# A segment-maximum stage whose TensorE makes the node positions one group earlier

## The reference, cut to what matters

```python
def _graph_conv(x, src, dst, ew, W_rel, b_rel, W_root):
    msg = x[src] * ew[:, None]
    agg = jax.ops.segment_max(msg, dst, num_segments=N)
    agg = jnp.where(jnp.isfinite(agg), agg, 0.0)
    return agg @ W_rel.T + b_rel + x @ W_root.T
src, dst = (edge_index[0], edge_index[1])
ew = 1.0 / (pos[src] - pos[dst])
```

## Time and profile before

| what | us |
|---|---|
| median of 3 runs | 6097.28 |
| lowest, highest | 6085.78, 6100.27 |
| the profiled execution, its device time | 6076.85 |
| its span, first to last instruction | 6075.1 |
| mean granted TensorE clock over the span | 0.720 |

### The profile page before, as it was taken

One profiled execution on the slowest core, in us unless ns is written; L12 is line 12 of the kernel. 1 busy time (PEld: TensorE's weight loads), 2 busy tenths in 40 slices (PEclk: granted clock), 3 DMA queues, 4 the chain that ended last, 5 costly groups with the idle time before them and its releaser, 6 DMA issues. The chain is left out here.

```text
span 6075.1 us, 87448 instructions
## 1 busy us (share of the span) xinstructions
PE 3609.1 (59%) x18318; PEld 2628.9 (43%) x18319; DVE 3319.1 (55%) x10385; ACT 1849.9 (30%) x4701; POOL 2684.2 (44%) x2677
## 2 busy tenths in 40 slices
PE   1455555555554454577214997995666666666664
PEld 0444454455532222244001554654555555555552
DVE  6666666666664444587001333225666666666668
ACT  0444444444422222243000000003444444444442
POOL 1555555555526666601774000005555455454524
PEclk9855555555566676687556998997777777777776
DMA  5555555556531111123103885644333333333331
GB/s 116 182 183 190 186 182 188 185 181 194 185 106 50 49 49 49 49 90 84 22 0 64 200 191 186 196 140 115 87 85 84 83 85 85 84 86 82 87 85 33
DMA packets 822107, 695.48 MB, mean 114 GB/s; under 512 B 538545, under 2 KB 717733, under 8 KB 808431
## 3 DMA queue, kind: packets, MB, share of 16 engines
q1 hardware_dynamic: 552746, 449.58, 24.9%
q0 software_dynamic: 97584, 175.68, 10.8%
q10 hardware_dynamic: 171540, 68.00, 4.7%
HBM read 510.64 MB, written 108.55 MB: 102 GB/s over the span
## 5 line engine op out<-in xcount | busy, mean ns | idle before, releaser
L2362 POOL DMA_INDIRECT ring<-xl_rows,idx x880 | 893.0, 1015 | 1681.1 <-DVE idx L2542 861.6
L435 POOL DMA_INDIRECT ringa<-x_sign_pos,idxa x880 | 864.7, 983 | 691.5 <-DVE msga L600 385.0
L987 POOL DMA_INDIRECT edge_counts<-edge_cnt,places x832 | 828.1, 995 | 733.9 <-issue 262.9
L520 PE MATMUL sela<-hota,endsa 128*128 128x128 f32 x1760 | 425.0, 417 | 482.6 <-ACT endsa L461 400.7
L1905 PE MATMUL pss<-x3s,mats 128*128 128x385 bf16 x2401 | 452.5, 340 | 355.3 <-issue 349.3
L2487 PE MATMUL zps<-xr,hotT 128*128 x2640 | 384.2, 254 | 381.1 <-DVE z L2561 212.6
L520 PEld LDWEIGHTS sela<-hota,endsa 128*128 128x128 f32 x1760 | 365.1, 307 | 500.5 <-issue 430.6
L2500 PE MATMUL ops<-val,hot 128*128 128x200 f32 x1760 | 469.6, 417 | 141.9 <-issue 125.5
L2683 DVE TENSOR_TENSOR out<-out,ops 128x200 f32 x880 | 317.9, 361 | 415.5 <-remote 277.0
L2489 PE MATMUL zps<-We,eaT 128*128 128x128 f32 x1760 | 495.3, 367 | 63.0 <-issue 62.4
L2487 PEld LDWEIGHTS zps<-xr,hotT 128*128 128x128 bf16 x2640 | 271.8, 114 | 492.1 <-issue 458.8
(11 more groups left out here) (388 smaller groups left out, 6591.7 us busy)
## 6 DMA issues: line engine op xcount, KB each, us to landing
edge_counts<-zeroa SPq DMA_DIRECT2D x55, 1568.0 KB
matd<-edge_counts SPq DMA_DIRECT2D x12, 6272.0 KB
keyb<-edge_keys SPq DMA_DIRECT2D x50, 1216.0 KB
reseta<-resets SPq DMA_DIRECT2D x110, 512.0 KB
dstba<-dst_in_tile_bf ACTq DMA_DIRECT2D x112, 256.0 KB
dstb<-dst_in_tile_bf SPq DMA_DIRECT2D x110, 256.0 KB
eaT<-in_eaT SPq DMA_DIRECT2D x880, 32.0 KB
val<-in_ea ACTq DMA_DIRECT2D x880, 32.0 KB
```

Source lines behind the costliest of these rows:

```text
L435: p.indirect_dma_start(out=ring[:, k, :], out_offset=None, in_=table, in_offset=bass.IndirectOffsetOnAxis(ap=idx[:, k:k + 1], axis=0)).the ...
L520: ins = t.matmul(sel[q % 2][:, k * P:(k + 1) * P], ends[:, q % 2, k, :], hot[:, q, k, :], start=True, stop=True)
L987: p.indirect_dma_start(out=g.M.rearrange("d s -> (d s)").unsqueeze(1), out_offset=bass.IndirectOffsetOnAxis(ap=g.place[:, c:c + 1], axis=0 ...
L2362: p.indirect_dma_start(out=ring[:, q % GR, k, :], out_offset=None, in_=g.xl_rows[0:N, :], in_offset=bass.IndirectOffsetOnAxis(ap=idx[:, (q ...
```

## The change

TensorE makes the positions of the next group in the middle of its iteration, between the selection and the transposes of messages, instead of those of the current group at its head. The positions of group 0 are made before the loop. One group of positions more is made at the end than is used.

```diff
@@ -543,10 +543,10 @@
                 def body(it):
                     for q in range(NG):
                         G = it * NG + q
-                        positions(G, q)
-                        for lag, stage in ((3, select), (1, transposed), (2, back)):
+                        for lag, stage in ((3, select), (-1, positions), (1, transposed), (2, back)):
                             if not (isinstance(it, int) and q < lag):
                                 stage(G - lag, (q - lag) % NG)
+                positions(0, 0)
                 turns(t, body, TURNS)
                 GL = TURNS * NG
                 select(GL - 3, NG - 3)
```

## The result

The changed kernel takes 6132.8 us (median of 6 runs, 6109.0 to 6150.7) and the kernel before, in the same comparison, 6096.7 us (6 runs, 6085.8 to 6100.3). The ratio is 1.006 with a 95% interval of 1.0037 to 1.0083: slower by about 36 us. So it is slower on all three occasions, by 0.35% to 0.6%.

A forecast was written before the change was run, and what follows sets the result against it. The prediction took the stage as bound by a loop of waits, VectorE's on four TensorE signals that come late while gathers run. Terms -49, +11 and +66 us gave +28 on 6097, so 6125 us; range over all 6025 to 6215.

The forecast's parts named there:

- The wait moves to the selection: VectorE's wait leaves the sum of positions (209.2 us) for the additions; additions plus scan grow from 177 to 300 us or more.
- -49 us for what stays gained: VectorE ahead of the sum of positions: 0.6 us comes back at each of 81 waits; bounds 0 and -138.
- +66 us for 20 long runs: GpSimd's gathers: 20 runs of twelve without a stop, TensorE's signals coming after their end, 3.3 us more each.
- +28 us of the sum: Whole program: the terms -49, +11 and +66 us together, added to the kernel before's time.
- +11 us for TensorE's loop: Position matmuls between selection and transposes put TensorE behind by about 0.1 us in half of 220 steps; bounds 0 and +64.
- GpSimd's waits: GpSimd's waits for messages, 101 for 385 us before, become fewer but longer, more of them near 8 us.
- need not stop: Messages come up to 3.45 us earlier after a long wait, so GpSimd goes on gathering without its stop.
- The clock: TensorE's granted clock, 0.58 in the stage, should stay; if it rose, all of TensorE's terms would shrink.
- (a): Rival: long gather runs do not get longer or cost nothing, sum -38 us, 6059 us; chance 0.22.
- (b): Rival: GpSimd's run and the held signals come 3.4 us earlier at some 45 waits, 153 us, 5944 us; chance 0.08.
- (c): Rival: no change, the wait moves whole to the selection or terms cancel, 6080 to 6115 us; chance 0.24.
- The rule of the Trainium skill: Spoke against the +66 us term: longer gather runs would hold nothing up, leaving a sum of -38 us.

The follow-up runs named there:

- second and third set: Later comparisons, each with its own kernel before (6017 and 6020 us); the changed kernel, run again unchanged, measured 1.0035 in both.
- experiment 4: Kernel before and changed kernel, each with the maximum stage's gathers left out after the first turn's 16: 0.9345 and 0.9329 of the whole kernel before.
- first set: Comparison of the later ring refill, doubled position matmuls and positions behind the transposes against the kernel before, which takes 6091 us there.
- later slots: Kernel before with the ring's slots filled one group later, GpSimd waiting for messages one group nearer: 1.0004 of the kernel before.
- two cut kernels: Kernel before and changed kernel with the maximum stage's gathers left out after the first turn's 16: 5621.1 and 5618.6 us.
- The same edit: Changed kernel with the ring's slots filled one group later: 0.9988, then 1.0022 of the kernel before.
- another 1.002 and 1.0056: Changed kernel with the next group's positions made behind the transposes of messages, ahead of the transposes back: 1.002, then 1.0056 of the kernel before.

## Why the prediction came out

The time was 6132.8 us where I had 6125 us, and slower by more than 0.3% was the likeliest case. The steps one by one:

- **The wait moves to the selection.** Right, though in part to the scan: 45 of the 247 us are ahead of it. Ahead of the sum of positions 1.5 us are left, as said (a few us). The additions and the scan together went from the 177 us of the earlier trace rows to 424 by the same rows after (220.1 + 119.9 + 84.3), past the 300 that I had named.
- **-49 us for what stays gained.** Open. By the booking the changed kernel gains 46 to 68 us in runs of 6 to 10 gathers, but that is a different thing from a gain at each wait, and no run has the gain without the rest. I had it from three waits walked; that the two numbers are near may be luck.
- **+66 us for 20 long runs.** The number was near: 15, 19 and 19 runs of eleven and more (with the one at the start left out), where there had been 2 and 4, so 13 to 15 more. The price was too high: such a run is booked at 3 x 0.70 to 3 x 0.78 = 2.1 to 2.3 us over three mean groups, and not 3.3, so 35 to 41 us. I had taken it from a single run at 8.29 us a group, and the mean is 7.74 to 7.94. That run was misread as well: after its first gather, leave out the next, which starts at 1642.49 after 2.05 us of idleness. So it was one gather, a pause, and eleven in a row. And since the kernel with positions made twice loses without long runs, that they cause the changed kernel's loss is not shown.
- **What the sum left out.** The short runs. Behind a run of eleven or twelve comes one of eight (48 of 53 times in the changed kernel's three traces), and behind that mostly one of four, with its own pause. Such short runs are booked at 17 us more in two profiles and 77 in one. Nothing in my sum stood for that. In the first profile it covered the price that was too high, and that is luck: the +28 us of the sum stands beside 36 measured there and 22 and 24 us in the second and third set, but its terms don't hold one by one.
- **+11 us for TensorE's loop.** Without gathers it is nothing: both orders take 1168 us. With gathers the doubled matmuls cost 14 to 29 us, so some of it may be real there. The two could not be told apart. The 482 us that the prediction gives as TensorE's wait for ScalarE's copy are all idle time ahead of the selection; the copy ends 401 of them. No term hangs on it.
- **GpSimd's waits.** Half right. They became longer: 29 are over 7 us, where 4 were. They did not become fewer: 107 against 101. So GpSimd stops as often as before; "need not stop" failed.
- **The clock.** 0.60 against 0.58, as expected no factor.
- **The rivals.** (a), faster by the gain alone, is out by the time. That long runs cost nothing, its reason, is not refuted as such: they take 7.7 to 8.1 us a group in every trace, in the kernel before too, but no edit tested their price. (b), the shorter loop, is out by its time, though runs of 6 to 10 did get shorter. (c), the same time, was close: 0.35% in the second and third set is just over the bound of 0.3%, which lies inside both intervals.
- **The rule of the Trainium skill**, page "SBUF — State Buffer", section "SBUF: two separate sides", that a DMA and a compute instruction don't slow each other: VectorE's times agree, as its scan takes 1275 ns with gathers and 1274 without. The eight matmuls of the selection are recorded with 2.07 us in both cases too, but their ends are modelled, so that is no test. But by that rule alone no signal of TensorE would come later for the gathers, and in experiment 4 the waits for these signals went away with them. Whether it is their writes to SBUF, their descriptors, the semaphores' own way or matmuls that really end later than the model says was not tried, and stays open.

What stays open besides is the rest of the program. In the first profiles it took 6128.9 - 1613.1 = 4515.8 us in the changed kernel and 4497.3 in the kernel before, 19 us more outside the stage, though nothing there was changed. The other profiles of the first set say the same: 4517 to 4522 us in the three that make positions early, and 4499 in the kernel before with later slots. In the second and third set the same difference was 1 to 9 us. For the two cut kernels it was 12 us between the profiled executions (spans 5629.0 and 5617.1 us, with stages alike), and yet the medians, 5618.6 and 5621.1 us, show none. So I can't say that it belongs to the program. It does mean that of the 36 us of the first comparison a part may lie outside the stage that the prediction is about.

## What to carry to other kernels

Here three orders on TensorE only chose which of its signals was waited for: where all signals of an engine are late at the same times, the wait taken away at one is met at the next. Before such a change, sum the waits for all signals of that engine (here 462 to 548 us of idleness ahead of positions, scan and additions in all twelve traces with gathers, whatever the order, of which 117 are not waits for a signal) and ask what they have in common. In a kernel that runs in a rhythm of long and short runs, the mean of a group hides a gain in one kind and a loss in another; reading it by runs finds them, but a cause needs an edit that sets the length of the runs alone. And repairs should be run in the same set as what they repair.

## What the runs showed that was not expected

Two loops that should take 5.3 us a group and less by themselves take 7.1 together. VectorE's with TensorE's is 5.31 us without gathers, which was measured. GpSimd's four gathers take 4 x (0.983 + about 0.3) = 5.1 us when nothing holds it, which is an estimate from the earlier trace rows. Together they take 1561.3/220 = 7.10 in the second profile of before. The 1.79 us between is 393 us in the stage, more than ten times what was moved here, and it goes with the signals of TensorE during gathers.

The same edit measured 0.9988 in one set (chip 11) and 1.0022 in another (chip 15), and another 1.002 and 1.0056, each with an interval of about 0.12% to 0.19% on either side. Each set's kernel before was its own yardstick. So a ratio from one set can be further from that of another than its interval says.
